# Attention scores in 32-key column tiles, and one stack cast a group later on ScalarE

## The reference

```
x = x + 0.5 * ffn(layernorm(x))
h = rmsnorm(layernorm(x)) ;  q = h @ Wq (4 heads of 32) ;  k, v = h @ Wk, h @ Wv (2 heads of 32)
q, k = l2norm(q), l2norm(k)
attn = softmax(where(causal, q k^T * exp(log_temperature), -inf))
x = x + [layernorm(x) + gate * (attn v) @ Wo]
x = x + 0.5 * ffn(layernorm(x))
```

## Time and profile before

| what | value |
|---|---|
| median of 3 runs | 447.22 us (447.05 to 448.2) |
| the profiled execution, its own time | 444.96 us |
| its span in the trace | 443.2 us |
| granted clock of TensorE over the span | 1.00 |
| busy: TensorE | 410.2 us, 93% |
| busy: VectorE | 357.3 us, 81% |
| busy: ScalarE | 372.7 us, 84% |
| busy: GpSimd | 254.9 us, 58% |

### The profile page before, as it was taken

The page is one execution under the profiler, slowest core; times in us unless marked ns, Lnnn a source line. Parts: engine busy times, 40 slices in busy tenths (PEclk is TensorE's granted clock), DMA queues, the critical chain, the costliest instruction groups (busy, mean ns, idle before and its releaser), DMA issues.

```text
span 443.2 us, 10510 instructions
## 1 busy us (share of the span) xinstructions
PE 410.2 (93%) x3747; PEld 215.0 (49%) x3747; DVE 357.3 (81%) x943; ACT 372.7 (84%) x513; POOL 254.9 (58%) x325
## 2 busy tenths in 40 slices
PE   0689998989998999999999999999999999999995
PEld 0346565664434435435335335336345245676654
DVE  5989997799789788888887898898768948888654
ACT  4799999776886978978978978978968998999960
POOL 5689999984634534534535435432232458999851
PEclk9999999999999999999999999999999999999999
DMA  6486443516336054054072072082070114476452
GB/s 166 111 188 154 50 60 60 96 22 121 51 71 122 1 106 89 0 99 94 0 130 59 0 142 50 1 138 54 1 143 1 25 26 96 95 119 122 104 112 76
DMA packets 119215, 34.95 MB, mean 79 GB/s; under 512 B 101632, under 2 KB 119168, under 8 KB 119168
## 3 DMA queue, kind: packets, MB, share of 16 engines
q1 hardware_dynamic: 117888, 34.02, 39.9%
q10 hardware_dynamic: 1280, 0.33, 0.3%
HBM read 4.98 MB, written 4.19 MB: 21 GB/s over the span
## 4 chain that ended last, share of the span: by engine, by line
PE 27%; ACT 24%; DVE 22%; issue 15%; POOL 6%; DMA 5%; SPq 0%; DVEq 0%; ACTq 0%
ACT PT L829 8%; ACT XN L459 6%; PE ps L716 6%; PE ps L723 5%; PE ps L696 5%; PE ps L507 4%; DVE RD L241 4%; ACT SG L477 3%; DVE RT L1059 2%; DVE H L328 2%; ACT w_int L470 2%; POOL HL L434 2%; DVE SS L1044 2%; PE ps L749 2%; DVE QN L1098 2%
## 5 line engine op out<-in xcount | busy, mean ns | idle before, releaser
L829 ACT ACTIVATE PT<-ps,k_exp 128x1024 f32<-128x1024 f32 (+1 forms) x160 | 155.9, 1040 | 12.2 <-PE ps L702 9.6
L507 PE MATMUL ps<-XT,WT 128*128 128x512 f16 x384 | 94.8, 386 | 5.6 <-DVE H L328 1.8
L696 PE MATMUL ps<-QKT 128*128 128x512 f16 (+3 forms) x384 | 87.1, 328 | 5.8 <-ACT PT L829 4.2
L716 PE MATMUL ps<-PT,V 128*32 128x512 f32 (+3 forms) x768 | 78.5, 496 | 0.0
L723 PE MATMUL ps<-PT,ones 128*32 128x512 f32 (+3 forms) x768 | 76.6, 486 | 0.0
L434 POOL TENSOR_TENSOR HL<-H,HH 128x1024 f16<-128x1024 f32 x31 | 66.6, 2147 | 8.3 <-ACT HH L483 5.3
L328 DVE SCALAR_TENSOR_TENSOR H<-SG,k_isilu,ps 128x1536 f32<-128x1536 f32 x32 | 57.8, 1807 | 13.9 <-ACT SG L477 6.4
L507 PEld LDWEIGHTS ps<-XT,WT 128*128 128x128 f16 x384 | 34.6, 99 | 50.7 <-issue 10.0
L696 PEld LDWEIGHTS ps<-QKT 128*128 128x128 f16 x384 | 27.8, 97 | 56.0 <-ACT PT L829 49.0
L459 ACT ACTIVATE XN<-X,NB,RS 128x128 f32<-128x128 f32 x128 | 52.4, 482 | 2.7 <-POOL NB L406 2.6
L282 POOL TENSOR_TENSOR OL<-ON,OH 128x512 f16<-128x512 f32 x15 | 17.6, 1173 | 60.9 <-ACT OH L278 60.9
(11 more groups left out here) (139 smaller groups left out, 647.4 us busy)
## 6 DMA issues: line engine op xcount, KB each, us to landing
result<-X SPq DMA_DIRECT2D x15, 256.0 KB, 2.5
X<-in_L_attn_x SPq DMA_DIRECT2D x7, 512.0 KB, 4.3
X<-in_L_attn_x SPq DMA_DIRECT2D x2, 256.0 KB, 4.9
XT<-w_int SPq DMA_TRANSPOSE x32, 3.1
QKT<-ST SPq DMA_TRANSPOSE x18, 5.6
AXT<-AS SPq DMA_TRANSPOSE x16, 2.8
w_int<-in_L_ffn_w_gate SPq DMA_DIRECT2D x1, 192.0 KB, 4.2
w_int<-in_L_ffn_w_up SPq DMA_DIRECT2D x1, 192.0 KB, 4.6
```

The source lines that it names most:

```text
L507: i = e.matmul(out[:, j, :], WT[:, wp, w * NJ + j, :], XT[k % 2][:, xp, :], start=a == 0, stop=a == len(passes) - 1)
L696: i_ = e.matmul(SCORES[hp][:, h, o:o + n], QKT[k % 2][:, i // TPC, NH + hp, i % TPC * P:(i % TPC + 1) * P], QKT[k % 2][:, qc, 2 * hp + h, ...
L716: e.matmul(PVD[HD * h:HD * h + HD, 0, CH - n:CH], V[k % 2][:, i, v0:v0 + HD], PT[g % 2][:, h, o:o + n], start=i == 0, stop=i >= TPC * qc, ...
L829: e.activation(PT[g % 2][:, 2 * hp:2 * hp + 2, 0:n], SCORES[hp][:, :, 0:n], ACT.Exp, scale=k_exp[:, 0:1]).then_inc(a_exp, 1)
```

## The change

Two edits. The first is in `scores`. For a key tile that needs no mask, each matmul with 128 stationary columns becomes four with 32 stationary columns each (32 keys), which write the four bands of 32 output partitions. The moving operand, the place of the keys in `QKT` and the result are as before. Per group and head pair there are 8 matmuls where there were 2. It applies to groups 3 to 6 of each batch. The second edit moves the stack cast of the second half, from step 5 to step 6 of a batch, for all batches but the first (where it stands in step 6 already).

```
                 for i, o, n in tiles_:
+                    keys = [slice(c, c + HD) for c in range(0, P, HD)] if i < TPC * qc else [slice(0, P)]
                     for h in range(2):
-                        i_ = e.matmul(SCORES[hp][:, h, o:o + n],
-                                      QKT[k % 2][:, i // TPC, NH + hp, i % TPC * P:(i % TPC + 1) * P],
-                                      QKT[k % 2][:, qc, 2 * hp + h, CH - n:CH], start=True, stop=True,
-                                      skip_group_check=o > 0)
+                        for c in keys:
+                            i_ = e.matmul(SCORES[hp][c, h, o:o + n],
+                                          QKT[k % 2][:, i // TPC, NH + hp, i % TPC * P + c.start:i % TPC * P + c.stop],
+                                          QKT[k % 2][:, qc, 2 * hp + h, CH - n:CH], start=True, stop=True,
+                                          skip_group_check=o > 0)
...
-                        g_ = g - 1 if k == 0 else g
-                        if g_ in (4, 5):
-                            stack_hi(m0 + (g_ == 5), int(g_ == 5))
+                        g_ = 4 if k else 5
+                        if g in (g_, 6):
+                            stack_hi(m0 + (g == 6), int(g == 6))
```

## The result

| | before | the change |
|---|---|---|
| median | 447.47 us (447.05 to 448.2, 4 runs) | 455.56 us (454.93 to 458.24, 4 runs) |
| profiled execution, its own time | 444.96 us | 455.01 us |
| span | 443.2 us | 453.2 us |
| granted clock over the span | 1.00 | 0.994 |

The ratio is 1.0191, with a 95% interval of 1.0146 to 1.0235. The kernel got slower by 8.1 us, where the forecast was slower by 4.3 us; the measured time lies just outside the range. The sign was right and the new ring is there, but a step takes more than the forecast gave it, and a fall of TensorE's clock comes on top.

What follows compares the result with a forecast made beforehand. It took a nearly closed ring of TensorE, ScalarE and VectorE as the bound: 5 x 1.1 = +5.5 us from the new ring, -1.2 from other batches, sum +4.3, giving 451.5 us; own range 450.3 to 454.5, stated range 446.3 to 455.5.

Steps and rivals of the forecast that it cites:

- new ring: Late cast, VectorE's copies, reciprocal, normalise, ScalarE's input casts, group 0, TensorE, group 7: 33.75 us a batch, 1.1 more, five batches.
- old ring: Squares, VectorE, wait for QN at the cast, group 7's exponentials, TensorE, reciprocal: 32.61 us a batch, cut by the second edit.
- first leg: From group 0's exponentials along TensorE to group 7's first scores: 22.13 us without gap, 0.20 less with the tiles.
- extra price of 0.04: Cost in us per group for the added matmuls and loads of 32-column tiles in groups 3 to 6; 0.16 a batch.
- the 0.09 saved twice: TensorE's cost in us per change between 32- and 128-column work; two fall away in groups 5 and 6, 0.36 a batch.
- third leg: From the late cast over VectorE and ScalarE's input casts to the next batch's group 0 exponentials: 9.82 us.
- same: Rival: VectorE's second copy parts from GpSimd's subtraction, the cast-to-group-0 leg shrinks by 0.9 us; 447.2 us, chance 0.17.
- the two exponentials: Second leg, on ScalarE from group 7's first scores to the late cast: 2.0 us.
- The -1.2 us of the other batches: Gains in the first, seventh and eighth batches, from vanished waits at group 8 and fewer shape changes: together -1.2 us.
- Faster: Rival: the leg from cast to group 0 doesn't bind, TensorE sets the pace at 32.08 us; 443.3 us, chance 0.12.
- The loads didn't bind: Rival that they do: unhidden 32-column weight loads cost 0.52 us for each of 32 groups; +21 us, 468, chance 0.06.
- the tiles ran at once: Rival that they don't at 16 bit: a group's scores take 3.5 us, 2.6 more, 32 times; 531 us, chance 0.02.

Runs made afterwards that it cites:

- e9: Kernel before with the column tiles and VectorE's reciprocal ahead of the copies, the cast where it was: 445.18 us, ratio 0.9982 to before.
- e1: Kernel before with only the second edit, the cast a group later, scores in 128-key tiles: 459.94 us, ratio 1.0299 to before.
- e5: The changed kernel with VectorE's reciprocal and product ahead of the two copies that wait for the late cast: 439.75 us, ratio 0.9855 to before.
- e3: The changed kernel with GpSimd's low part of the normalised input (L957) waiting until normalise has ended: 450.75 us, ratio 1.011 to before.
- e8: The changed kernel with eight unused matmuls in TensorE's wait, second to sixth batch: 453.41 us, ratio 1.016 to before.
- e7: e1 with eight unused 128x512 matmuls in TensorE's wait for group 0's exponentials, second to sixth batch: 454.59 us, ratio 1.0165 to before.
- e10: The changed kernel run once more, unaltered, beside e4 on one chip: 457.63 us, ratio 1.0257 to before.
- e4: The changed kernel with both GpSimd subtractions (L282 and L957) waiting until normalise has ended: 446.92 us, ratio 1.0034 to before.

## Why the prediction was right and wrong

**The old ring and its end.** Right. Group 7's exponentials start right after its scores, the wait for QN is gone (ScalarE's waits for it fell from 12.2 to 5.2 us; 4.0 of these stand ahead of the loop and 1.2 in the first batch, where the cast was not moved), and e9 shows that this ring holds as long as the cast is not moved.

**The new ring.** Right in every link; e1 shows that the second edit alone closes it, and e5 that the reciprocal behind the late cast is the link to cut.

**Its first leg, less 0.20 for the tiles.** About right. From group 0's exponentials to group 7's first scores it was to be 21.93 us; with 34.31 a batch it is 195.81 - 174.13 = 21.68. The tiles' part is measured by e1 against the change, 34.48 - 34.31 = 0.17 a batch. The leg without tiles was read too long: it is 231.47 - 209.62 = 21.85 in e1, not 22.13. TensorE "has no gap" there, but its weight loads waited for ScalarE, 0.43 and 0.48 us at the second pairs of groups 4 and 5, and ScalarE had waited 0.52 us for VectorE's product (its cast at 179.60). In e1 that cast (218.54) has no wait, and those of the loads are gone at group 4 and 0.27 us at group 5. How the tiles' part comes about was wrong in detail: a set of 16 has no extra price of 0.04 (219.45 - 218.58 = 0.87, against 0.88), and in groups 5 and 6 the 0.09 saved twice is mostly turned into a wait for ScalarE.

**The third leg, 9.82 us, "all of it work or waiting for that work".** This is the step that failed. I took the leg from the trace as if its durations were fixed, and it was 10.57. With the cast late, ScalarE had been through group 9's exponentials when the product came, so its cast of it (L278) and GpSimd's subtractions followed at once. A second one then fell on `normalise` and held it 0.75 us. I had weighed the hold of the copy at this very place (the rival "same"), and not asked the same question of `normalise`, which had one hold in it already. e3 shows that this is the step: with the second hold taken away the leg is 9.73. The term was 1.1 us a batch and measured 34.31 - 32.61 = 1.70: over five batches 8.5 for 5.5. The three legs account for it: +0.75 on this one, -0.25 on the first, +0.06 on the two exponentials between (197.87 - 195.81 = 2.06) make the 0.56 by which 34.31 exceeds the 33.75 of the forecast.

**The -1.2 us of the other batches.** About right: from the last squares to the last cast of the attention's output it is 369.63 - 327.13 = 42.50 us, where it was 359.75 - 316.09 = 43.66. With it the ring costs 7.3 us, which is what e8 shows (1.6% of 446.62 is 7.1).

**What I had not in the sum at all** is TensorE's clock. I wrote that TensorE would wait 1 to 2 us in each of five batches, and gave that no price beyond the ring. It waited 2.46, and after some of these waits the granted clock fell to 0.50, the 1.2 GHz level, for part of the next stretch, in which TensorE is the first leg of the ring. One fall cost 1.5 us in the profiled execution of the change; e1 had four. With 7.3 for the ring that makes 8.8 of the 10.05 us by which the two profiled executions differ. The rest is small and spread: the last of before's five batches took 32.22 us and not 32.61, 0.7 us come ahead of the second batch (154.10 for 153.43) and 0.1 behind the attention.

**The rivals.** "Same" needed the copy to part from GpSimd's subtraction; it did not (1.18 us at 198.95). "Faster" needed the leg from the cast to group 0 below 8.15 us. e5 gets the whole of it: with the leg cut, 31.81 a batch and 1.5% less than before. The loads didn't bind and the tiles ran at once; no run shows a cost of the slower load that the Trainium skill's rule on Fast Weight Load ("TensorEngine Tiling (Array Packing)", Restrictions) lets one expect.

## What to carry to other kernels

When a wait is moved down a queue, follow everything that is queued behind the moved instruction on the other engines until the walk comes back to where it began, and add up the legs: here the wait that was removed had been worth 1.17 us and the ring that replaced it was 1.7 longer. Treat durations taken from a trace as valid only for the neighbours they had: ask of each VectorE operation on the path which GpSimd operation runs beside it now. And before giving up an edit that opens a new ring, look for the one operation in it that needn't be there; the move that lost 1.9% gains 1.5% once the reciprocal no longer stands behind the cast.

## What the runs showed of the hardware that I had not expected

- Eight matmuls of 128x512 whose results nobody reads, put into a wait of TensorE, go with a kernel that is about 6 us faster (e1 and e7, on two chips), and the granted clock of the profiled execution is 0.998 instead of 0.984. After waits of about 2.5 us the clock fell in some batches and not in others (once in five in the change, three times in e10, four times in e1), from run to run differently, so that the runs of e1 spread over 3.5 us and those of e10 over 5.9. Shorter waits don't exclude it: the traces have one fall each after a wait of 1.60 us (e3, at 273 us), 1.73 us (e9, at 141 us) and 2.06 us (e5, at 114 us), and even before had runs at 0.994 to 0.996 that took 446.5 to 448.7 us. None of the traces has a fall after the loop's waits of 0.73 us (e8) or 1.23 us (e4).
- A weight load of 32 columns at 16 bit takes 95 ns in the table by form, one of 128 columns 98 ns. So a load of a quarter of the columns is no cheaper, and sixteen of them behind a set of tiles cost nothing that shows: the set takes 0.87 us, four whole scores took 0.88.
- One VectorE operation of 0.34 us that meets a GpSimd subtraction takes 1.2 us (1.18 and 1.19 in the change). Eight in a row take 2.13 us undisturbed, 2.98 to 3.08 with one meeting and 3.83 with two.
